# A macaron layer on one core: a rewritten opening, and VectorE's order where a turn begins

## What is computed

```python
x = x + 0.5 * ffn(layernorm(x))
x = x + attn(layernorm(x))
x = x + 0.5 * ffn(layernorm(x))

def ffn(x):                       # w1, w2: 512x128, h1, h2: 512x512, w3: 128x512, ternary weights
    h = silu((x @ w1.T) * s1) * ((x @ w2.T) * s2)
    h = gelu((h @ h1.T) * t1)
    h = gelu((h @ h2.T) * t2)
    return (h @ w3.T) * s3

def attn(x):                      # 16 states
    xB = x @ B
    h = scan(lambda h, xb: tanh(xb + h @ A.T), 0, xB)
    return (h @ C) @ W_out.T + b_out
```

## Time and profile before

| | us |
|---|---|
| median of 3 runs (403.16 to 404.03) | 403.85 |
| profiled execution, its own time | 403.09 |
| span in its trace | 400.8 |
| PE busy | 384.4 (96% of the span) |
| DVE, ACT, POOL busy | 275.9, 270.6, 165.4 |

### The profile page before, as it was taken

One profiled execution on the slowest core, in us unless ns is written; L12 is line 12 of the kernel. 1 busy time (PEld: TensorE's weight loads), 2 busy tenths in 40 slices (PEclk: granted clock), 3 DMA queues, 4 the chain that ended last, 5 costly groups with the idle time before them and its releaser, 6 DMA issues.

```text
span 400.8 us, 6692 instructions
## 1 busy us (share of the span) xinstructions
PE 384.4 (96%) x1789; PEld 301.4 (75%) x1789; DVE 275.9 (69%) x729; ACT 270.6 (68%) x641; POOL 165.4 (41%) x156
## 2 busy tenths in 40 slices
PE   6769999999999999999999999999999999999995
PEld 4546787787878878777777777878778787877773
DVE  4794677767775776676787866776767577676713
ACT  3557767686877868678475685857577675747663
POOL 3433546262555526245262453524235352433421
PEclk9898999999999999999999999999999999999999
DMA  7910000000000000000101001010100101010001
GB/s 261 430 45 2 1 26 2 28 2 1 28 1 26 0 26 0 0 28 1 52 2 53 2 1 52 2 53 2 48 5 0 52 0 52 0 53 0 2 27 30
DMA packets 6219, 13.97 MB, mean 35 GB/s; under 512 B 1072, under 2 KB 1840, under 8 KB 5936
## 3 DMA queue, kind: packets, MB, share of 16 engines
q1 hardware_dynamic: 5184, 13.37, 8.6%
q10 hardware_dynamic: 1008, 0.29, 0.3%
HBM read 7.37 MB, written 2.10 MB: 24 GB/s over the span
## 4 chain that ended last, share of the span: by engine, by line
PE 82%; DVE 7%; ACT 3%; issue 3%; POOL 2%; DMA 1%; DVEq 0%; POOLq 0%; ACTq 0%
PE F L261 67%; PE FR L261 8%; PE FR L289 2%; DVE xnt_f L698 1%; POOL rs_f L1320 1%; PE SC L402 1%; DVE st_f L665 1%; DVE u L710 1%; DVE y L720 1%; PE MI L289 1%; PE MI L269 1%; DMA x_all<-in_xtok 1%; ACT xnt_f L1112 1%; ACT th L1055 1%; POOL w_lo L1377 1%
## 5 line engine op out<-in xcount | busy, mean ns | idle before, releaser
L261 PE MATMUL F<-y_hi,w_hi 128*128 128x512 f32 x509 | 210.3, 413 | 4.3 <-DVE y_lo L735 1.8
L261 PE MATMUL F<-y_lo,w_hi 128*128 128x512 f32 x509 | 201.3, 396 | 0.0
L261 PEld LDWEIGHTS F<-y_hi,w_hi 128*128 128x128 f32 x509 | 96.0, 189 | 28.8 <-issue 6.6
L261 PEld LDWEIGHTS F<-y_lo,w_hi 128*128 128x128 f32 x509 | 96.3, 189 | 18.2
L1073 ACT ACTIVATE y<-F,sc 128x512 f32<-128x512 f32 x110 | 75.3, 684 | 44.8 <-PE F L261 44.3
L740 DVE TENSOR_TENSOR y_lo<-y,y_hi 128x512 fp32r<-128x512 f32 x79 | 64.7, 819 | 50.6 <-ACT y_hi L1076 50.6
L1325 POOL TENSOR_TENSOR y_lo<-y,y_hi 128x512 fp32r<-128x512 f32 x48 | 67.9, 1417 | 64.1 <-DVE y_hi L727 53.6
L1331 POOL TENSOR_TENSOR y_lo<-y,y_hi 128x512 fp32r<-128x512 f32 x48 | 62.1, 1300 | 35.4 <-ACT y_hi L1076 35.4
L1076 ACT ACTIVATE y_hi<-F,sc 128x512 fp32r<-128x512 f32 x110 | 75.1, 683 | 0.0
L1092 ACT ACTIVATE h<-SC 128x32 fp32r<-128x32 f32 x104 | 20.3, 195 | 55.6 <-PE SC L417 53.8
L261 PE MATMUL F<-xn_hi,w_hi 128*128 128x512 f32 x119 | 50.6, 425 | 2.4 <-POOL w_lo L1377 1.9
(11 more groups left out here) (134 smaller groups left out, 405.6 us busy)
## 6 DMA issues: line engine op xcount, KB each, us to landing
x_all<-in_xT SPq DMA_DIRECT2D x1, 2048.0 KB, 17.1
x_all<-x1c SPq DMA_DIRECT2D x8, 256.0 KB, 2.3
x_all<-lnin SPq DMA_DIRECT2D x8, 256.0 KB, 2.3
out<-outb SPq DMA_DIRECT2D x7, 256.0 KB, 2.0
x_all<-in_xtok SPq DMA_DIRECT2D x1, 1536.0 KB, 12.7
w_raw<-in_h1T SPq DMA_DIRECT2D x2, 512.0 KB, 7.7
w_raw<-in_h2T SPq DMA_DIRECT2D x2, 512.0 KB, 9.5
x_all<-in_xtok SPq DMA_DIRECT2D x2, 256.0 KB, 4.7
```

The costliest lines, as they stand in the source:

```text
L261: mm = nc.tensor.matmul(out, wtile(w, layer, k, m), y, start=first and i == 0, stop=last and i == len(pairs) - 1)
```

## The change

Two things are rewritten. In the opening, PE runs more dummies (19, and two behind the first transposes); layer 1 of chunk 0 begins with the products that need only `xn_hi`, and `w_lo` comes in two halves; layer 2 does all four outputs for k = 0, 1, 2 and the rounded part of k = 3 ahead of the branch, so that four matmuls with `y1_lo` of k = 3 are left behind it. DVE's order follows: the statistics of chunk 1 stand behind the first gate, `low1(0)` stands among the counts, `mix_parts` (constants for the scan) goes behind the branch and its last three into turn 1, and DVE normalises chunk 2 in place of ACT. Bank F[4] takes the transposes of chunk 1 in place of F[3], so that F[3] can take the fourth output of layer 2; the count's sum goes to SC.

At a turn's edge, `low1` leaves `end_turn` and stands in the next turn: first of all in the early turns and the last, behind `attention` in the middle and late ones. In those, `layer4` goes behind `front_stats`.

```diff
-WARM = 13
+WARM = 19
...
+        def turned(g):
+            return 0 if isinstance(g, int) and g <= 1 else g - 2
...
-                        pe.wait_ge(y1_r, m + 3)
+                        pe.wait_ge(u_r, m + 3)
                         pe.wait_ge(y2_hi_r, m)
...
+            def first_layer1():
+                out = l1_banks(0, 0)
+                w = [[wtile(part, layer, 0, 0) for part in (w_hi, w_lo)] for layer in (0, 1)]
+                pe.wait_ge(w_hi_ready, 2)
+                pe.wait_ge(xn_hi_r, 1)
+                for b in range(2):
+                    nc.tensor.matmul(out[b][:, :], w[b][0], xn_hi[:, :], start=True, stop=False)
+                pe.wait_ge(w_lo1_ready, 1)
+                for b in range(2):
+                    nc.tensor.matmul(out[b][:, :], w[b][1], xn_hi[:, :], start=False, stop=False)
+                pe.wait_ge(xn_lo_r, 1)
+                for b in range(2):
+                    nc.tensor.matmul(out[b][:, :], w[b][0], xn_lo[:, :], start=False, stop=False)
+                    mm = nc.tensor.matmul(out[b][:, :], w[b][1], xn_lo[:, :], start=False, stop=True)
+                mm.then_inc(l1_mm, 1)
+
+            def first_layer2(k):
+                pe.wait_ge(y1_hi_r[k], 1)
+                if k < KT - 1:
+                    pe.wait_ge(y1_lo_pool, k + 1)
+                for m in range(KT):
+                    w = wtile(w_hi, 2, k, m)
+                    nc.tensor.matmul(B2[m][:, :], w, y1_hi[:, k, :], start=k == 0, stop=False)
+                    if k < KT - 1:
+                        nc.tensor.matmul(B2[m][:, :], w, y1_lo[:, k, :], start=False, stop=False)
...
             def first_turn(gen):
+                pe.wait_ge(y1_lo_dve, 1)
...
+                    nc.tensor.matmul(B2[m][:, :], wtile(w_hi, 2, KT - 1, m), y1_lo[:, KT - 1, :], start=False,
+                                     stop=True).then_inc(l2_mm, 1)
                 layer1(1, 0, gen)
+                layer1(1, 1, gen)
                 pe.wait_ge(w_hi_ready, len(PIECES))
-                first_layer2(KT - 1, range(KT), gen, finish=True)
-                layer1(1, 1, gen)
                 layer3(0, 0, gen)
...
+            zeros(2)
+
+            first_layer1()
+            layer1(0, 1, True)
+            pe.wait_ge(w_lo1_ready, 2)
+            layer1(0, 2, True)
+            layer1(0, 3, True)
...
@@ def end_turn(g):
                 gated(g + 1, KT - 1)
                 y1_high(g + 1, KT - 1)
-                low1(g + 1)
                 low(g, 3, y3_hi_r, y23, y3_hi, y3_lo, y3_lo_dve)
...
@@ def middle_turn(g, c):
                     attention(c - 1, c - 1)
+                    low1(g)
+                    front_stats(g + 1)
                     layer4((g - 1) // CHUNKS, g - 1, (g - 1) % CHUNKS)
-                    front_stats(g + 1)
...
@@ def _(act):
-            gelu2(0, 0)
-            gelu2(0, 1)
-            gelu2(0, 2)
-            normalise(2)
+            for m in range(KT):
+                gelu2(0, m)
             layer1(1, 0)
-            gelu2(0, 3)
...
@@ def _(pool):
-            pool.tensor_tensor(w_lo[:, 0:WOFF[2]], w_raw[:, 0:WOFF[2]], w_hi[:, 0:WOFF[2]].bitcast(F32),
-                               ALU.subtract).then_inc(w_lo1_ready, 1)
+            for half in range(2):
+                part = [w[:, 0:WOFF[2]].rearrange("p (l n) -> p l n", l=2)[:, :, half * HID // 2:(half + 1) * HID // 2]
+                        for w in (w_lo, w_raw, w_hi)]
+                pool.tensor_tensor(part[0], part[1], part[2].bitcast(F32), ALU.subtract).then_inc(w_lo1_ready, 1)
```

More of the change, by code:

```diff
@@ L458, in early_turn, with zeros @@
                 to_features("f", xnt_f, FR, g + 2)
[L460 to L472, removed]
+            def zeros(n):
+                for _ in range(n):
+                    nc.tensor.matmul(SC[:, :], y3_lo[:, 0, 0:P], y3_lo[:, 0, :], start=True, stop=True)
@@ L476, in first_turn @@
                 if gen:
                     pe.wait_ge(w_lo_ready, 1)
-                for m in range(KT - 1):
+                for m in range(KT):
                     if gen:
-                        first_layer2(m, range(KT - 1), True, high=False)
-                    first_layer2(m, [KT - 1], gen, finish=True)
+                        for k in range(KT):
+                            w = wtile(w_lo, 2, k, m)
+                            nc.tensor.matmul(B2[m][:, :], w, y1_hi[:, k, :], start=False, stop=False)
+                            nc.tensor.matmul(B2[m][:, :], w, y1_lo[:, k, :], start=False, stop=False)
+                    nc.tensor.matmul(B2[m][:, :], wtile(w_hi, 2, KT - 1, m), y1_lo[:, KT - 1, :], start=False,
+                                     stop=True).then_inc(l2_mm, 1)
@@ L623, in _ @@
             pe.wait_ge(zeros_set, 1)
-            for _ in range(WARM):
-                nc.tensor.matmul(SC[:, :], y3_lo[:, 0, 0:P], y3_lo[:, 0, :], start=True, stop=True)
+            zeros(WARM)
             pe.wait_ge(ld_id, 16)
@@ L629, in _ @@
             nc.tensor.matmul(F[0][:, 0:P], ct[:, :], wout[:, :], start=True, stop=True).then_inc(cw_mm, 1)
[L631 to L634, removed]
+            zeros(2)
[4 more added lines that the diff above has]
+            layer1(0, 3, True)
             pe.wait_ge(cw_ready, 2)
             pe.wait_ge(w_hi_ready, 4)
[L637 to L641, removed]
+            first_layer2(0)
+            pe.wait_ge(u_r, 3)
+            to_features("f", xnt_f, F[4], 1)
+            first_layer2(1)
+            first_layer2(2)
             pe.wait_ge(ne_ready, len(PIECES) + 1)
             pe.wait_ge(set_up, 1)
-            pe.wait_ge(y1_r, 3)
-            nc.tensor.matmul(F[4][0:1, 0:1], ne_sum[:, :], ones[:, :], start=True, stop=True).then_inc(gen_mm, 1)
+            pe.wait_ge(u_r, 4)
+            nc.tensor.matmul(SC[0:1, 0:1], ne_sum[:, :], ones[:, :], start=True, stop=True).then_inc(gen_mm, 1)
+            first_layer2(3)
             pe.wait_ge(gen_ready, 2)
@@ L815, in step @@
                         scan_low(scan, t)
+                    if scan is None and t in (1, 2, 3):
+                        mix(t - 1)
+                low1(g)
                 xn_low(g + 1)
```

75 lines of the change are left out of this document (39 added, 36 removed).

## The result

The changed kernel took 397.51 us (median of 4 runs, 396.95 to 398.47) and the kernel before, beside it, 403.86 us (4 runs, 403.16 to 404.03): a ratio of 0.986, 95% interval 0.9842 to 0.9877. Forecast were 396.2 us and 7.6 us of gain; it was 6.35. The profiled execution took 397.82 us with a span of 395.8, against 403.09 and 400.8.

The account below looks back on a forecast made before the run. The opening was taken as bound by a chain over all engines, the turns by PE's work with small stalls. Opening 5.4 + turns 2.2 = 7.6 us, so 403.85 − 7.6 = 396.2 us; range 394.4 to 397.5, wider 394.2 to 399.3.

Parts of the forecast that it names:

- Steps 1 and 2: Opening: split layer 1 brings DVE's first gate to 12.7 us, 2.7 us earlier; the extra dummies cost 0.1 us.
- Step 3: Opening, DVE's queue: work leaving and entering cancels at 1.9 us each; `general` comes 3.0 us earlier, at 25.6 us.
- rival A: Opening: DVE and GpSimd hold each other up ahead of `general`; gain 6.4 down to 4.8 us, around 397.8; chance 0.17.
- Step 4: Branch: `general` to PE's first matmul behind it takes 1.3 us, so that starts at 26.9 us, 3.3 us earlier.
- Steps 5 and 6: Opening after the branch: ACT does only gelus, layer 3 starts at 32.2 us; the stream starts 5.8 us earlier.
- Step 7: PE's new 2.4 us wait before layer 3 may lower the clock: 0 to 0.9 us, taken 0.4, leaving 5.4.
- The turns: Middle and late turns: removing PE's stalls at `front_tokens`, `to_features` and the last `y3_lo` gains 2.2 us, ceiling 2.6.
- rivals B: Turns give nothing back, a new wait replacing the old; only the opening's 5.4 us counts: 398.4 us; chance 0.12.
- C: Slower: in eight middle and late turns PE waits for `layer4` behind the statistics; 406.4 at 1 us a turn; chance 0.05.
- D: Opening does not move, because of something unpriced, and the turns give under 0.8 us: 403.5 us; chance 0.05.
- the forecast as computed: Whole kernel: the steps' and turns' sum with its own range, 394.4 to 397.5 us; chance 0.61.

Follow-up runs that it names:

- x8_no_two: The changed kernel without the two dummy matmuls between the product with w_out and layer 1: 397.64 us, against 397.42 us for the changed kernel.
- x4_fill: The changed kernel plus eight dummy matmuls in PE's gap ahead of layer 3 of chunk 0: 396.67 us median over ten runs with this fill, against 397.42.

## Why the forecast was right, and 1.3 us off

For the profiled pair (403.09 and 397.82 us, 5.27 us apart), by the steps of the prediction:

- **Steps 1 and 2, first gate.** 13.08 for 12.7 us. Layer 1 started at 10.23 us because the weights of the output product landed at 9.4, and the gate waits for the tanh behind it (0.38 us). Close behind stands a second limit: the count of the second piece took 1.28 us beside GpSimd's `w_lo`, where the estimate had no hold-up, and DVE's counts end at 12.7 us; in `x8_no_two` they set the gate. The clock stayed up. 0.4 us short.
- **Step 3, `general`. This is the step that failed.** It said "the two cancel" and took off 0.3 us for less waiting. From the gate to `general` it was 13.23 us before and is 13.73: 0.8 us worse than forecast, and 1.2 us with step 1. The 1.1 us by which `low1(0)` is held up stand in the middle of it. (DVE's queue before was not "nearly full" either: it held a wait of 1.00 us for `w_hi`, which ended at 20.61 us and is gone, so less waiting was worth more than 0.3 us and hid a part of the hold-up.) They are rival A's mechanism, but not quite at rival A's price: with `low1(0)` gone from there, or the held one replaced, only 0.4 us comes back, since GpSimd's own late `y_lo` sets PE's sum next. Rival A saw DVE's side alone. What `general` would do if GpSimd's side were freed too was not tried.
- **Step 4.** From `general` to the first matmul behind the branch 1.26 us, for 1.3.
- **Steps 5 and 6.** First gelu 0.53 us behind that matmul (0.5 forecast), layer 3 4.83 us later (4.8), then the stream. Where the clock doesn't fall, `general` to the stream is 10.1 us, for 10.3 forecast. The normalise on DVE took 2.13 us and not 1.1, beside GpSimd's `y_lo`, and was hidden all the same.
- **Step 7, the clock.** The right mechanism and the wrong size: 0.4 us taken, bound 0.9, and 1.3 when it falls. Up to the stream it cost 0.9 us (`general` to the stream is 11.04 us, and 10.1 where the clock stays up), which is the bound; the bound left out the chain that the slow matmuls delay into turn 1. It also falls in only a part of the executions.
- **Turn 1, a term that the prediction put at nothing.** The last three mix instructions moved there. The first two are cheap; the third stands beside two `y_lo` of GpSimd (54.52, 2.54 us) and takes four times as long:

```profile
53.60 0.34 DVE L820 SCALAR_TENSOR_TENSOR cw_mix<-part_lo,mask,part_own 128x128 fp32r<-128x128 f32 x1
...
55.86 1.35 DVE L820 SCALAR_TENSOR_TENSOR cw_mix<-part_lo,mask,part_own 128x128 fp32r<-128x128 f32 x1
```

  The gates behind it come late, and with them PE's `xn_hi` group. From `to_features` of the scan's input in turn 1 to the next `to_features` it takes 10.57 us, and 10.42 before: 0.15 us. In ten of the eleven other profiles with the new opening (all but `x4_fill`) it is 10.83 to 10.86, a loss of 0.4 us. So this is rival A's mechanism a second time, and no run moved the instruction away.
- **The turns.** 3.2 us for 2.2, over the ceiling of 2.6. In turns 7, 8 and 9 I took the stretched step, 0.39 for 0.23 us. The steps behind it, at 192.10, were longer too (0.31 and 0.27 us); each of these stalls was worth 0.27 or 0.28 us up to the start of the transposes and not 0.16, and the transposes themselves brought another 0.06. The loop gave 1.7 of the 1.8 us forecast, the turn behind it 0.38 for 0.3, and none of the 0.1 us a turn left out was lost. `layer4` behind the statistics held nothing up: rivals B and C are out, and D with them, since the opening moved by 3.9 us.
- **The end.** Not in the prediction at all: 1.4 us, for code that no one runs.

The sum: 7.6 − 1.2 − 0.9 − 0.15 + 1.0 − 1.4 = 4.95 us, where the pair has 5.27; 0.2 us of the rest are steps 5 and 6. The medians have 6.35 because the pair was unlucky by 1.1 us: the execution of before was 0.76 us under its median, that of after, with a fall of the clock, 0.31 us over its own.

The time came out right partly by luck. The turns gave 1.0 us more than forecast, about what steps 1 and 3 lacked, and 1.4 us went at a place that neither the forecast nor a rival named. 397.51 us lies on the edge of the forecast as computed (394.4 to 397.5) and beside rival A's 397.8; but at A's place only 0.8 of its 1.2 us were lost, and the rest of that agreement is chance.

## What to carry to other kernels

Where two engines can shut each other out of a memory, look at what each of them has running at the same time on both sides of the chain, and put beside the other engine's work an instruction that has been seen to run there at its own speed. Here that was the statistics. One input is not enough: the normalise took 2.13 us for 1.1 beside GpSimd's `y_lo`, and two casts at 40.17 us took 1.72 for 0.84. Moving the victim only passes the wait to its neighbour. Price a fall of the clock up to the next point at which the other engines catch up, and fill a gap of 2 us in PE's stream with dummies if nothing needs PE then. After every change of an engine's code compare the last instructions of all engines, since the end of the span can move for reasons that no computation has.

## What the runs showed of the hardware

- The granted clock fell behind a gap of 2.31 us in PE's work in four of six profiles, and behind the same gap it stayed at 1.00 in the other two. The prediction named a page of the Trainium skill (TensorE: Matmul & The Clock Gate, section Why this matters for your kernels) that warns only of longer ones; the runs stand against it.
- A late last instruction on DVE, 1.8 to 2.3 us behind engines that waited on the same semaphores, comes or goes with the number of instructions ahead of it: 1.4 us of time for eight memsets that never run. It then stands 1.28 to 1.40 us behind the end of an instruction packet that starts 0.6 us behind DVE's drain in every profile.
- GpSimd's `y_lo` is held for 1 us by a DVE count that started 0.1 us ahead of it, and in the same place a DVE `y_lo` or count is held for 1.1 us by GpSimd. DVE's statistics, with one input, are not (0.87 us); its normalise and its casts, with one input too, are (2.13 for 1.1 us, 1.72 for 0.84), and so is a mix instruction of 128x128 (1.35 for 0.34).
